# Own-attention maxima from padded keys, nine exponential buffers and a new order of the attention stage

## The reference, cut to what matters

```python
def _attn(x, ctx, wq, wk, wv, wo, bo, heads):
    q = (x @ wq).reshape(b, n, heads, dh).transpose(0, 2, 1, 3)
    k = (ctx @ wk).reshape(b, j, heads, dh).transpose(0, 2, 1, 3)
    v = (ctx @ wv).reshape(b, j, heads, dh).transpose(0, 2, 1, 3)
    a = jax.nn.softmax(jnp.einsum('bhid,bhjd->bhij', q, k) * scale, axis=-1)
    out = jnp.einsum('bhij,bhjd->bhid', a, v)
    return out.transpose(0, 2, 1, 3).reshape(b, n, heads * dh) @ wo + bo
h1 = _ln(x, n1_g, n1_b);  x = _attn(h1, h1, q1, k1, v1, o1_w, o1_b, heads) + x
h2 = _ln(x, n2_g, n2_b);  x = _attn(h2, context, q2, k2, v2, o2_w, o2_b, heads) + x
h3 = _ln(x, n3_g, n3_b);  a, g = jnp.split(h3 @ ff_w1 + ff_b1, 2, axis=-1)
return (a * gelu(g)) @ ff_w2 + ff_b2 + x
```

## Time and profile before

| what | value |
|---|---|
| time, median of 3 runs | 1338.87 us (1338.45 to 1339.19) |
| the profiled execution's own time | 1340.0 us |
| its span | 1338.2 us |
| PE busy | 1293.6 us (97%), 13364 matmuls |
| DVE busy | 825.6 us (62%) |
| ACT busy | 680.7 us (51%) |
| POOL busy | 616.9 us (46%) |
| mean granted clock of TensorE | 0.992 |

### The profile page before, as it was taken

One profiled execution on the slowest core, in us unless ns is written; L12 is line 12 of the kernel. 1 busy time (PEld: TensorE's weight loads), 2 busy tenths in 40 slices (PEclk: granted clock), 3 DMA queues, 4 the chain that ended last, 5 costly groups with the idle time before them and its releaser, 6 DMA issues. The chain is left out here.

```text
span 1338.2 us, 35594 instructions
## 1 busy us (share of the span) xinstructions
PE 1293.6 (97%) x13364; PEld 1204.0 (90%) x13364; DVE 825.6 (62%) x1729; ACT 680.7 (51%) x1558; POOL 616.9 (46%) x723
## 2 busy tenths in 40 slices
PE   6999789999999999999999999999889999999999
PEld 4999779999999899999899999997689999999999
DVE  5645377777777787777777777776665334252421
ACT  4665245566565566565565565565553232313131
POOL 5521234654654654654654654644356242333331
PEclk9999799999999999999999999999899999999999
DMA  4676645445445455455445445442111101010000
GB/s 124 226 253 217 201 124 151 137 130 164 122 131 156 150 151 175 139 149 177 136 135 155 127 128 161 124 139 95 42 54 49 45 1 49 0 49 0 24 1 25
DMA packets 118995, 154.59 MB, mean 116 GB/s; under 512 B 22336, under 2 KB 112696, under 8 KB 118840
## 3 DMA queue, kind: packets, MB, share of 16 engines
q1 hardware_dynamic: 118840, 152.49, 37.3%
HBM read 62.98 MB, written 28.93 MB: 69 GB/s over the span
## 5 line engine op out<-in xcount | busy, mean ns | idle before, releaser
L1398 ACT ACTIVATE probs<-expin 120x400 f32<-120x400 f32 (+2 forms) x635 | 311.4, 506 | 157.4 <-PE expin L753 101.7
L1075 DVE TENSOR_REDUCE neg_max<-score 100x2 f32<-100x722 f32 x320 | 290.1, 907 | 53.5 <-PE score L727 41.2
L1584 POOL MEMSET qs<- 1x2400 f32 (+1 forms) x116 | 224.2, 1933 | 33.9 <-PE attn L776 26.1
L753 PE MATMUL expin<-qs,ks 128*120 128x200 f32 (+2 forms) x1270 | 234.6, 275 | 3.9 <-ACT probs L1398 1.7
L753 PEld LDWEIGHTS expin<-qs,ks 128*120 128x120 f32 (+2 forms) x1270 | 190.8, 179 | 22.5 <-issue 9.1
L727 PE MATMUL score<-ks,qs 128*100 128x362 f32 x640 | 165.4, 339 | 5.3 <-DVE neg_max L1075 4.8
L2594 DVE SCALAR_TENSOR_TENSOR hidden<-ps_a,b_cols,gelu 128x320 f32<-128x320 f32 x100 | 55.0, 550 | 163.7 <-PE ps_a L2518 159.2
L2756 POOL TENSOR_TENSOR hid_lo<-hidden,hid_hi 128x320 fp32r<-128x320 f32 x100 | 89.2, 892 | 120.6 <-ACT hid_hi L2664 120.4
L2676 ACT ACTIVATE gelu<-ps_g,b_cols 128x320 f32<-128x320 f32 x100 | 52.8, 528 | 134.4 <-PE ps_g L2518 134.4
L1612 POOL TENSOR_TENSOR ctx_hi<-ctx_raw,one 128x480 fp32r<-128x480 f32 (+1 forms) x62 | 49.0, 791 | 128.8 <-PE work L693 114.7
L166 DVE TENSOR_REDUCE neg_max<-score 100x10 f32<-100x1000 f32 x62 | 74.4, 1200 | 47.3 <-PE score L159 47.3
(11 more groups left out here) (220 smaller groups left out, 3048.7 us busy)
## 6 DMA issues: line engine op xcount, KB each, us to landing
ks<-kc_parts SPq DMA_DIRECT2D x192, 181.0 KB, 3.0
qk_dram<-qk_parts SPq DMA_DIRECT2D x32, 500.0 KB, 5.3
qs<-q_parts SPq DMA_DIRECT2D x192, 75.0 KB
ks<-qk_dram SPq DMA_DIRECT2D x96, 125.0 KB
ctx_raw<-in_ctxT SPq DMA_DIRECT2D x64, 180.5 KB
ks<-kc_parts SPq DMA_DIRECT2D x96, 90.5 KB, 2.2
qs<-qk_dram SPq DMA_DIRECT2D x64, 125.0 KB
v_dram<-v_rows SPq DMA_DIRECT2D x32, 132.8 KB
```

Source lines behind the costliest of these rows:

```text
L753: mm = pe.matmul(dst, ks[a][u][:, c, j0:j0 + n], qs[a][u][:, :, q_slot(c) if a == 2 else c, :], start=True, stop=True)
L1075: ins = nc.vector.tensor_reduce(dst, src, AX_X, ALU.max, negate=True)
L1398: nc.scalar.activation(probs[e % NPT][0:n, :], expin[e % 2][0:n, 0:HG * N], ACT.Exp, scale=SCALE)\
L1584: link(nc.gpsimd.memset(row, 0.0))
```

## The change

The own products for the maxima swap the padding. The keys are padded by head and the queries are dense, so that one matmul has the dense queries of a pair as weights and both heads' padded keys as 200 moving columns (dense_products). The dense queries are loaded to a tensor of their own (own_q). The keys for the exponentials stay dense (ks[1]). The padded keys (in the place of the old qs[1][1]) and the padded queries (own_pad, in the place of the old qs[1][0]) exist once and are made by POOL, by two copies of 64 partitions each (spread_keys, spread_queries). Samples 0 to 2 keep the old form. x2 is one tensor instead of two, and the exponential buffers go from eleven to nine. The orders of PE, DVE, ACT, POOL and SP change, as do the orders of the work banks. Cut to the core:

```diff
-NW, NPT = 3, 11
+NW, NPT = 3, 9
-    order = [("KC", c, 0), ("OX1", c, 0), ("MT1", f, 0), ("OX1", c, 1), ("KC", c, 1), ("OT1", c, 0), ("KC", c, 2),
+    order = [("KC", c, 0), ("KC", c, 1), ("OX1", c, 0), ("MT1", f, 0), ("OX1", c, 1), ("KC", c, 2), ("OT1", c, 0),
...
+def load_dense(sp, b, qk1_dram, v1_dram, keys, vs, landed):
+    src = qk1_dram[b]
+    k = src[:, 64:P].rearrange("l (r b) m -> l r (b m)", b=2)
+    for slot, part in enumerate((0, 0, 1)):
+        sp.dma_start(keys[product_rows(slot)].rearrange("p c n -> p (c n)").bitcast(F32), k[part]).then_inc(landed, 16)
+    sp.dma_start(vs[:].rearrange("p h d -> p (h d)"), v1_dram[b]).then_inc(landed, 16)
+def load_dense_queries(sp, b, qk1_dram, queries, landed):
+    q = qk1_dram[b][:, 0:64].rearrange("l (r b) m -> l r (b m)", b=2)
+    dst = queries[1:P:2].rearrange("p c n -> p (c n)").bitcast(F32)
+    sp.dma_start(dst, q[0].unsqueeze(1).broadcast_to([32, 2, HP * N])).then_inc(landed, 16)
+    sp.dma_start(queries[product_rows(1)].rearrange("p c n -> p (c n)").bitcast(F32), q[1]).then_inc(landed, 16)
+def dense_products(pe, banks, queries, keys, i):
+    half = HP // 2
+    for k in range(half):
+        c = half * i + k
+        first = 2 * k // half
+        if (2 * k + 1) // half == first:
+            at = 2 * k % half * N
+            dst = banks[0:N, first, at:at + 2 * N].rearrange("p (a n) -> p a n", a=2)
+            mm = pe.matmul(dst, queries[:, c, :], keys[:, :, c, :], start=True, stop=True)
+        else:
+            for a in range(2):
+                at = (2 * k + a) % half * N
+                mm = pe.matmul(banks[0:N, first + a, at:at + N], queries[:, c, :], keys[:, a, c, :], start=True, stop=True)
+    return mm
...
-        x2 = two("x2", [N, D])
+        x2 = sb("x2", [N, D])
+        own_q = sb("own_q", [P, HP, N], F32R)
+        own_pad = at("own_pad", [P, HP, 2, N], own[0])
...
 load_qkv1:
+                load_dense(sp, b, qk1_dram, v1_dram, ks[1][u], vs[u], qkv1_landed[u])
+                    sp.wait_ge(score_full, SCORE_AT[1, b - 1, 1] + 1)
+                    sp.wait_ge(queries_spread, b - 3)
+                load_dense_queries(sp, b, qk1_dram, own_q, qkv1_landed[u])
 place_max:
+                if a == 1 and b > 2:
+                    sp.wait_ge(queries_spread, b - 2)
+                    store_max(sp, own_pad, max_parts[1], max_landed[1][u])
 SP period:
+                load_context(f)
                 load_x(f)
+                load_qkv1(e)
                 place_max(1, f)
-                load_context(f)
-                load_qkv1(e)
                 place_kc(c, 0)
                 place_kc(c, 1)
+                place_kc(c, 2)
                 place_q2(c)
                 place_max(2, s)
                 store_x2(x)
-                place_kc(c, 2)
 self_scores and scores_for_exp:
+                        pe.wait_ge(keys_spread, b - 2)
+                    dense_products(pe, score, own_q, qs[1][1], i).then_inc(score_full, 1)
+                moving = own_pad[:, c] if a == 1 and b > 2 else qs[a][u][:, :, q_slot(c) if a == 2 else c, :]
 PE run_out:
                 scores_for_exp(2, 29, 4, 0)
+                times_v(2, 29, 1)
...
-                times_v(2, 29, 1)
 PE period:
                 scores_for_exp(1, c, 0, 0)
+                scores_for_exp(1, c, 1, 0)
                 self_scores(f, 0)
-                scores_for_exp(1, c, 1, 0)
+                project_kc(c, 0)
                 scores_for_exp(1, c, 2, 0)
-                project_kc(c, 0)
+                project_kc(c, 1)
                 scores_for_exp(1, c, 3, 0)
                 self_scores(f, 1)
...
                 scores_for_exp(2, x, 1, 1)
-                project_kc(c, 1)
+                project_kc(c, 2)
                 scores_for_exp(2, x, 1, 2)
+                scores_for_exp(2, x, 2, 0)
                 cross_scores(s, 2)
-                scores_for_exp(2, x, 2, 0)
+                times_v(2, x, 0)
+                times_v(2, x, 1)
                 turn_heads(1, c)
-                project_kc(c, 2)
...
                 scores_for_exp(2, x, 3, 1)
-                project_vc(c, 0)
+                times_v(2, x, 2)
                 scores_for_exp(2, x, 3, 2)
                 scores_for_exp(2, x, 4, 0)
+                project_vc(c, 0)
+                scores_for_exp(2, x, 4, 1)
                 cross_scores(s, 5)
-                times_v(2, x, 0)
-                times_v(2, x, 1)
-                times_v(2, x, 2)
-                scores_for_exp(2, x, 4, 1)
-                cross_scores(s, 6)
                 scores_for_exp(2, x, 4, 2)
                 turn_normalised(c)
                 times_v(2, x, 3)
                 times_v(2, x, 4)
+                cross_scores(s, 6)
                 project_q2(c)
 DVE period (kc_low(c, 1) and kc_low(c, 2) one place earlier too):
                 maximum(2, s, 3)
-                kc_low(c, 2)
+                second_input(c)
                 maximum(2, s, 4)
-                second_input(c)
+                normalise(c)
                 maximum(2, s, 5)
-                normalise(c)
+                features_low("T2", c)
                 maximum(2, s, 6)
-                features_low("T2", c)
 POOL:
+            def spread(halves, rows, step):
+                for a, half in enumerate((slice(0, 64), slice(64, P))):
+                    link(nc.gpsimd.tensor_copy(halves[a], rows[half].bitcast(F32)))
+                pool.sem_inc(step, 1)
+            def spread_keys(b):
+                pool.wait_ge(qkv1_landed[b % 2], own_landed(b))
+                pool.wait_ge(score_full, SCORE_AT[1, b - 1, 1] + 1)
...
+                spread([qs[1][1][64 * a:64 * a + 64, a] for a in range(2)], ks[1][b % 2], keys_spread)
+            def spread_queries(b):
+                e = EXP_AT[1, b - 1, G - 1, 0]
+                pool.wait_ge(exp_full[e % 2], e // 2 + 1)
...
+                spread([own_pad[64 * a:64 * a + 64, :, a] for a in range(2)], own_q, queries_spread)
 POOL lead_in, at its end:
+                spread_keys(3)
 POOL period:
-                clear_own(p + 4 if p + 4 < B else None)
+                spread_queries(f)
+                first_residual(f)
                 inverse_deviation(c)
-                first_residual(f)
+                spread_keys(p + 4 if p + 4 < B else None)
                 second_residual(c)
                 split_context(f)
                 clear_cross(c)
```

More of the change, by code:

```diff
@@ L101, in load_own, with own_landed, dense_maximum @@
     sp.dma_start(vs[:].rearrange("p h d -> p (h d)"), v1_dram[b]).then_inc(landed, 16)
-OWN = 9
+OWN, DENSE = 9, 6
+def own_landed(b):
+    padded = 2 if b % 2 == 0 else 1
+    return 16 * (OWN * (min(b, padded) // 2 + 1) + DENSE * (max(b - padded, 0) // 2))
+def load_dense(sp, b, qk1_dram, v1_dram, keys, vs, landed):
[23 more added lines that the diff above has]
+    return mm
+def dense_maximum(nc, neg_max, banks, i):
+    n = HP // 2
+    src = banks[0:N, :, 0:n * N].rearrange("p a (c j) -> p a c j", c=n)
+    dst = neg_max.rearrange("p a c -> p (a c)")[:, HP * i:HP * (i + 1)].rearrange("p (a c) -> p a c", a=2)
+    return nc.vector.tensor_reduce(dst, src, AX_X, ALU.max, negate=True)
 OWN_STEPS = [("scores", 0), ("scores", 1), ("max", 0)] + [("exponents", g) for g in range(G)]
@@ L400, in attention_phase @@
         pv = {1: pv1, 2: sb("pv2", [P, G * N])}
-        x2 = two("x2", [N, D])
-        more = [sb(f"probs{i}", [JT[2][1], HG * N]) for i in range(G, G + 2)]
+        x2 = sb("x2", [N, D])
+        own_q = sb("own_q", [P, HP, N], F32R)
+        own_pad = at("own_pad", [P, HP, 2, N], own[0])
+        sb("own_room", [P, 120])
+        more = []
         assert 32 * math.ceil(nc.sbuf_base / 32) == floor + PROBS_AT, (nc.sbuf_base - floor)
         sb("probs_room", [P, HG * N * G + 504 + 3 * P])
-        more += [sb(f"probs{i}", [JT[2][1], HG * N]) for i in range(G + 2, G + 5)]
+        more += [sb(f"probs{i}", [JT[2][1], HG * N]) for i in range(G, G + 3)]
         assert 32 * math.ceil(nc.sbuf_base / 32) == floor + INPUT_AT, (nc.sbuf_base - floor)
         sb("input_room", [P, 2 * D + 3 * 728])
-        more += [sb(f"probs{i}", [JT[2][1], HG * N]) for i in range(G + 5, NPT)]
+        more += [sb(f"probs{i}", [JT[2][1], HG * N]) for i in range(G + 3, NPT)]
         probs = probs + more
@@ L517, in place_max @@
                 sp.wait_ge(*emptied((f"MT{a}", b, 0)))
-                if b > (2 if a == 1 else 1):
-                    last = EXP_AT[a, b - 2, G - 1, 0 if a == 1 else 2]
+                if a == 1 and b > 2:
+                    sp.wait_ge(queries_spread, b - 2)
+                    store_max(sp, own_pad, max_parts[1], max_landed[1][u])
+                    return
+                if a == 2 and b > 1:
+                    last = EXP_AT[2, b - 2, G - 1, 2]
                     sp.wait_ge(exp_full[last % 2], last // 2 + 1)
@@ L752, in scores_for_exp @@
                     dst = expin[e % 2][0:n, i * 2 * N:(i + 1) * 2 * N].rearrange("p (a n) -> p a n", a=2)
```

(10 more changed lines are left out.)

59 lines of the change are left out of this document (34 added, 25 removed).

## The result

| what | before | after |
|---|---|---|
| median of the runs | 1339.03 us (4 runs, 1338.45 to 1342.81) | 1353.59 us (4 runs, 1350.79 to 1361.64) |
| the profiled execution's own time, span | 1340.0, 1338.2 us | 1351.3, 1349.5 us |
| ratio after / before | | 1.0109, 95% interval 1.0084 to 1.0133 |

The changed kernel is 1.1% slower. The forecast was 0.3% faster, and 1353.59 lies above both of its ranges (1330 to 1340, and for 8 in 10 up to 1350).

What follows compares the result with a forecast made beforehand. TensorE's issue, busy 97% of the span, was taken as the bound. -0.17 us a period over 29 periods (-4.8), with -1.0, +1.3 and +0.5, gave -4.0: 1334.9 us against the median; range 1330 to 1340, 8 in 10 1326 to 1350.

Steps and rivals of the forecast that it cites:

- Own products: TensorE's own products as twelve matmuls, not twenty: a half takes 0.58 us, saving 0.60 us a period.
- The normalised input: Chain from statistics through rstd and z to TensorE's transpose T2: TensorE waits 0.10 us a period, between 0.04 and 1.16.
- GpSimd's total: Four copies come and two clears go on GpSimd, 55% busy; its idle time covers this, costed at 0.
- SP's queue: SyncE issues 29 DMAs a period, not 31; place_q2 and place_max(2, s) are not delayed; gain of 1 us in all.
- Values in three pieces: TensorE's cross values in three pieces instead of two: one more piece costs 0.33 us a period, bounds 0.155 to 0.4.
- z behind the key copy: VectorE's z stands still until GpSimd's first key copy is through; TensorE then waits 0.10 us a period at T2.
- c: Time of one GpSimd key copy, 64 partitions x 1000 elements: taken as 1.0 us, between 0.936 and 2.06.
- A: Rival, slower: z waits behind a longer key copy, from 1.17 us on; 1349 at 1.5, 1365 at 2.06; chance 0.26.
- B: Rival: TensorE does not wait at T2, as the copy is short or z runs alone; 1332 or 1327; chance 0.20.
- C: Rival, no change: the saved 0.60 us comes back where TensorE waits for VectorE's maxima; 1338 to 1340; chance 0.18.
- The nine buffers: Nine exponential buffers hold back two more exponentials in the run-out: 1.3 us once, 0 to 2.5.
- the lead-in: Before the periods, spread_keys(3) stands behind the last split of the context: 0.5 us once, 0 to 4.1.

Runs made afterwards that it cites:

- before_pool: The kernel before with only GpSimd's two steps swapped, first_residual(f) ahead of inverse_deviation(c): 1339.40 us, ratio to before 0.9995.
- before_sp: The kernel before with only SyncE's order changed, load_context(f) ahead of load_x(f), both ahead of place_max(1, f): 1340.66 us, ratio to before 1.0006.
- inv_first: The changed kernel with one swap on GpSimd, inverse_deviation(c) ahead of first_residual(f): 1333.84 us against 1339.36 for the kernel before, ratio 0.9956.
- x_first: The changed kernel with load_x(f) ahead of load_context(f) on SyncE, GpSimd's order as changed: 1336.19 us, ratio to the kernel before 0.9976.
- own_twenty: inv_first with each sample's own products written as twenty matmuls of 100 columns again: 1354.92 us, ratio to the kernel before 1.0110.
- four_pieces: z_alone with cross_scores(s, 6) between the values of groups 3 and 4, so cross values stand in four pieces, not three: 1340.29 us.
- values_joined: inv_first with the cross values in two pieces again, groups 0 and 1 moved back to group 2's place: 1342.56 us, ratio to the kernel before 1.0011.
- z_alone: inv_first with GpSimd also waiting for z of sample c between inverse_deviation(c) and first_residual(f): 1331.43 us, ratio to the kernel before 0.9933.
- before_both: The kernel before with both moved steps: context loaded ahead of x on SyncE, first_residual(f) ahead of inverse_deviation(c) on GpSimd: 1404.40 us, ratio 1.0459.

## Why the prediction was wrong

**The step that failed** stands in *The normalised input*: "After the change the instruction behind rstd is no longer that residual but the first key copy of spread_keys." I asked only what now stands behind rstd, since that decides how long z takes. I did not ask where the residual had gone. It had gone ahead of inverse_deviation, with its wait for the load of x, and GpSimd works in order. *GpSimd's total*, which I costed at 0, was an argument about busy time (55%) and says nothing about who waits behind whom. *SP's queue* has the other half: I counted the time of issues for place_kc and place_q2, and not when x lands with the context ahead of it. Each half alone costs nothing that can be seen, as before_pool and before_sp show in the kernel before, and inv_first and x_first in the changed one; the pair costs 15.9 us in the profiled execution of the changed kernel, in ten periods that the prediction never told apart from the rest.

**Own products**, -0.60 forecast: a half takes 0.54 to 0.55, and own_twenty gives 0.62 a period. Right.

**Values in three pieces**, +0.33: four_pieces gives 0.29 for one piece more: 0.12 in the values and 0.08 in each of the two neighbours shown, where the forecast had 0.155, 0.08 and 0.09. About right, with the reserve that the neighbours' share may be the waits for the maximum, of up to 0.17. That a piece can be joined again at no cost was no part of the prediction, and values_joined shows that it can't be here.

**z behind the key copy**: c is 1.02 us (forecast 1.0), z ends at 4.01 (forecast 3.98), T2 starts at 4.07 (715.83) and waits 0.20, since TensorE gets there at 3.87 in z_alone (325.31 to 329.18); the forecast was 0.10, from 4.04 and 3.94. The price of the copy against nothing is 24.83 - 24.59 = 0.24 a period, against the forecast 0.10. Right in kind, too small by more than half. From the 1.03 cycles an element of the Trainium skill (GPSIMD Engine Reference, "Elementwise — side-by-side cycle accounting") the prediction had an estimate of 0.86 for the copy; the trace shows 1.02, and the measurement decides.

**The sum.** inv_first is the change with the failed step put back. It is 5.5 us faster than before (1333.84 against 1339.36) where the sum had -4.0 (its 29 x -0.17 is -4.9 and not -4.8, a slip of 0.1). A period without z's wait is 0.33 shorter than before (24.92 to 24.59), forecast 0.27.

**The rivals.** A named a time near the one that came (1349 at c = 1.5), but that is luck. Its sign came too, waits of TensorE for z over 0.2 (0.99 to 2.84 in the ten periods), but from another cause, for z took 0.48 there. c was 1.02, and with x early the copy costs 7 us in all (29 x 0.24). B's 1332 is what z_alone shows, 1331.43: with z alone TensorE does not wait for it in the periods. C's mechanism did not show in the changed kernel, where from 205 to 895 us no row has TensorE wait for a maximum; it is what took values_joined's gain.

**Not settled.** The nine buffers and the lead-in. From the first own product of the last period to the last store of x2 the kernel before takes 87.7 us, the changed one 89.2, inv_first 90.7 and z_alone 87.4. The last three have the same nine buffers and differ among themselves by more than the +1.3 forecast. The granted clock of this stretch is 0.96, 0.96, 0.94 and 1.00 in the four profiled executions, so the lengths hold differences of the clock as well; no run here shows the +1.3 of the buffers or the +0.5 of the lead-in by itself. And the four runs of the changed kernel spread over 11 us, with a mean granted clock of 0.983 in the slowest against 0.991 in the profiled one. 0.008 of 1360 us would be 11, an estimate from these two clocks; what lowered the clock is not shown, for no trace of that run is there.

## What to carry to other kernels

When an instruction moves on an in-order engine, list its waits, and everything that it moves ahead of now waits for them too; a wait of 9 us on an engine that is half idle is harmless or not by the one instruction behind it. Put the short links of the critical chain (here two instructions of 100 elements) ahead of whatever waits for a transfer, and look at the periods one by one: a mean of 25.4 hid eighteen at 24.8 and ten at 26.4. When a split or a join of a series is priced, ask also what the series was keeping apart.

## What the hardware showed that I had not expected

- x, 125 KB, landed 6.5 us after its issue began in the period without w1 that was read, 9.6 behind w1 and the context, and 6.4 (441.31 to 447.74) behind w1 alone. Its issue on SyncE took 1.55 us behind both, where 0.49 is usual.
- A stall can cost more than its length: after 4.22 us of idle in before_both TensorE's granted clock was 0.73, 0.50 and 0.86 over the next 5.6 us, and the period grew by 6.0. Behind 2.84 us in the changed kernel it stayed at 1.00.
- One wait on GpSimd, which only delays what GpSimd does, took 2.4 us off the median (inv_first to z_alone; the two intervals overlap, the mean period of 24.75 and 24.66 says the same), because VectorE's z went from 0.96 to 0.48 us.
